# Values and denominators of the last head group moved to the head of TensorE's iteration, and the keys' lower halves made and written earlier

## The reference

```
xn  = layernorm(x)
q, k, v = relu(xn), relu(ctx), relu(ctx)            # 16 heads of 32 features
o   = softmax(q @ k.T / sqrt(32)) @ v
x   = x + tanh(g_xattn) * relu(o @ ffn_w.T + ffn_b)
xn  = layernorm(x);  xp = xn shifted by one token
r   = sigmoid((mu_r*xn + (1-mu_r)*xp) @ W_r)
k_  = relu((mu_k*xn + (1-mu_k)*xp) @ W_k) ** 2
out = x + tanh(g_ffn) * r * (k_ @ W_v)
```

## Time and profile before

| what | value |
|---|---|
| median of 3 runs | 2935.4 us (2933.75 to 2940.07) |
| the profiled execution, its time | 2935.97 us |
| its span | 2934.1 us |
| PE busy | 2833.1 us (97%) |
| PE weight loads busy | 2183.8 us (74%) |
| DVE busy | 2349.9 us (80%) |
| ACT busy | 1568.1 us (53%) |
| POOL busy | 1044.8 us (36%) |
| mean DMA rate | 139 GB/s |

### The profile page before, as it was taken

One profiled execution on the slowest core, in us unless ns is written; L12 is line 12 of the kernel. 1 busy time (PEld: TensorE's weight loads), 2 busy tenths in 40 slices (PEclk: granted clock), 3 DMA queues, 4 the chain that ended last, 5 costly groups with the idle time before them and its releaser, 6 DMA issues. The chain is left out here.

```text
span 2934.1 us, 71298 instructions
## 1 busy us (share of the span) xinstructions
PE 2833.1 (97%) x23168; PEld 2183.8 (74%) x23168; DVE 2349.9 (80%) x4175; ACT 1568.1 (53%) x2828; POOL 1044.8 (36%) x902
## 2 busy tenths in 40 slices
PE   3899999999999999999999999999999999999998
PEld 2677777777777777777777777777777777777776
DVE  5788888888888878878878878888888888888874
ACT  4455555555555555555555555555555555555552
POOL 0233333343343333333343333333333333333333
PEclk9999999999999999999999999999999999999999
DMA  5544545535445445445445445445445455355431
GB/s 167 153 129 145 154 121 151 155 121 154 151 123 156 143 127 159 138 130 159 138 131 159 133 138 155 129 145 153 126 147 156 121 152 154 122 154 149 126 104 42
DMA packets 405258, 408.56 MB, mean 139 GB/s; under 512 B 164577, under 2 KB 329441, under 8 KB 405218
## 3 DMA queue, kind: packets, MB, share of 16 engines
q1 hardware_dynamic: 352994, 340.92, 39.7%
q10 hardware_dynamic: 52224, 67.12, 7.0%
HBM read 272.64 MB, written 134.22 MB: 139 GB/s over the span
## 5 line engine op out<-in xcount | busy, mean ns | idle before, releaser
L699 DVE TENSOR_REDUCE m_nat<-bank 128x2 fp32r<-128x512 f32 x1024 | 694.6, 684 | 142.0 <-PE bank L906 141.5
L477 ACT ACTIVATE q_st<-bank 96x512 fp32r<-96x512 f32 x512 | 303.9, 593 | 765.7 <-PE bank L875 765.7
L496 ACT ACTIVATE probs<-bank 128x512 f32<-128x512 f32 x1024 | 593.6, 590 | 195.8 <-PE bank L918 187.2
L718 DVE RECIPROCAL o_val<-bank 128x256 f32<-128x256 f32 x256 | 449.3, 1755 | 60.4 <-PE bank L944 53.2
L918 PE MATMUL bank<-q_st,k_st 97*128 97x256 f32 x2048 | 437.9, 295 | 18.3 <-DMA q_st<-m_t 18.1
L906 PE MATMUL bank<-k_st,q_st 96*128 96x256 f32 x2048 | 430.0, 292 | 6.0 <-DMA k_st<-k_dram 4.5
L918 PEld LDWEIGHTS bank<-q_st,k_st 97*128 97x128 f32 x2048 | 345.5, 190 | 84.5 <-issue 22.6
L906 PEld LDWEIGHTS bank<-k_st,q_st 96*128 96x128 f32 x2048 | 356.8, 192 | 58.1 <-issue 5.9
L364 POOL TENSOR_TENSOR o_lo<-o_mv,o_hi 128x512 fp32r<-128x512 f32 x128 | 174.0, 1360 | 583.3 <-ACT o_hi L503 583.3
L397 POOL TENSOR_TENSOR xm<-xm 128x512 f32<-128x512 f32 x128 | 137.6, 1075 | 637.0 <-ACT xm L540 637.0
L708 DVE CAST m_t<-bank 4x256 fp32r<-4x256 f32 x256 | 105.1, 411 | 286.2 <-PE bank L884 286.1
(11 more groups left out here) (90 smaller groups left out, 5893.6 us busy)
## 6 DMA issues: line engine op xcount, KB each, us to landing
k_st<-k_dram SPq DMA_DIRECT2D x256, 256.0 KB, 3.6
k_raw<-ctx_t_dram SPq DMA_DIRECT2D x256, 128.0 KB, 3.1
x_ln<-x_dram SPq DMA_DIRECT2D x256, 128.0 KB
k_dram<-k_high SPq DMA_DIRECT2D x64, 512.0 KB, 3.0
k_dram<-k_raw SPq DMA_DIRECT2D x64, 512.0 KB, 4.5
k_st<-k_dram SPq DMA_DIRECT2D x256, 128.0 KB, 3.5
o_dram<-o_val SPq DMA_DIRECT2D x256, 128.0 KB, 1.7
o_mv<-o_dram SPq DMA_DIRECT2D x512, 64.0 KB, 2.0
```

Of the source, the lines that this page charges most:

```text
L477: nc.scalar.activation(q_st[0:QK, c, :, P * u:P * u + P], tp_bank[0:QK, :].rearrange("p (g t) -> p g t", g=GR), ACT.Copy).then_inc(q_stack ...
L496: nc.scalar.activation(probs[:, n // GR % 2, n % GR, :, :].rearrange("p v t -> p (v t)"), st_bank[n % 2][:, :], ACT.Exp, scale=SCALE).then ...
L699: nc.vector.tensor_reduce(m_nat[:, c % 2, :, n % GR:n % GR + 1], s_bank[n % 2][:, :].rearrange("p (u y) -> p u y", u=NU), AX_X, ALU.max, n ...
L718: nc.vector.reciprocal(o_val[:, :], pv_bank[:, T:2 * T]).then_inc(rden_ready, 1)
```

## The change

On TensorE, `values(i - 1, 3)` and `denominators(i - 1, 3)` move from around `turn(1)` into the iteration's first step, on both sides of `scores(i, 7)`. On DVE, `norm_o(i - 1, 3)` and `copy_m(i, 1)` change places, and `k_low(i + 2)` moves from the end of the iteration to the step behind `copy_m(i + 1, 0)`. On SP, `write_k(i + 2)` moves ahead of `read_o(i, 0)` and `write_o(i, 2)`. Nothing is added or removed.

```diff
@@ SP
                 move_m(i + 1, 0)
                 load_w(i)
+                write_k(i + 2, par)
                 read_o(i, 0)
                 write_o(i, 2)
-                write_k(i + 2, par)
@@ DVE
                 head_max(i, 7)
                 finish(i - 3, 1, 1 - par)
+                norm_o(i - 1, 3)
                 copy_m(i, 1)
-                norm_o(i - 1, 3)
                 mix_r(i - 2)
@@ DVE
                 head_max(i + 1, 3)
                 copy_m(i + 1, 0)
+                k_low(i + 2)
 
                 head_max(i + 1, 4)
                 stats_1(i + 2)
@@ DVE
                 head_max(i + 1, 6)
-                k_low(i + 2)
@@ TensorE
                 dense(0, 0)
+                values(i - 1, 3)
                 scores(i, 7)
+                denominators(i - 1, 3)
                 dense(0, 1)
 
                 shifted_scores(i, 1)
-                values(i - 1, 3)
                 turn(1)
-                denominators(i - 1, 3)
                 dense(0, 2)
```

## The result

The changed kernel takes 3004.97 us (median; 3003.48 to 3005.99, four runs), and the kernel before 2934.57 us beside it. The ratio is 1.0236 with a 95% interval of 1.0218 to 1.0254: 70 us slower, where 64 were forecast against the time before (3000.0 less 2936.0). The profiled execution's span is 3001.6 us instead of 2934.1.

A forecast was written before the change was run, and what follows sets the result against it. PE, busy 97% of the span, was taken to bound the kernel. 2936.0 + 112.9 (two waits) - 45.3 (`o_low`) - 4.4 (start) - 0.7 (end) + 1.5 (iteration 1) = 3000.0 us; range 2982 to 3018, 8 in 10 2965 to 3020.

The forecast's parts named there:

- First wait: PE's values would wait for DVE's `norm_o(i - 1, 2)`, delayed by the early `k_low`: 0.8 us an iteration.
- Second wait: PE's `turn(2)` would wait for DVE's `copy_m(i, 1)`, now queued behind `norm_o(i - 1, 3)`: 0.9 us an iteration.
- Borders: On PE, `scores(i, 7)` standing alone between two float32 pieces would cost 0.15 us an iteration.
- The wait that goes: PE's recurring wait for `o_low` ahead of `dense(3, 0)` would go: a gain of 45.3 us.
- SP's order: `read_o(i, 0)` behind `write_k` would cost nothing; without cover, `turn(1)` would wait for `q_st`, 1 us each making 61 us.
- Start and end: First scores at 24.1, gaining 4.4 us; last wait shrinking by 0.7; iteration 1 paying 1.5.
- The stated bounds: Range of 2982 to 3018 us, with both waits at their bounds and the start's gain open.
- Only one wait: Rival: unseen DVE slack removes one of the two PE waits, giving 2945 us; chance 0.07.
- Neither: Rival: neither PE wait on DVE shows and the kernel is faster, 2895 us; chance 0.05.
- `o_low` stays: Rival: PE's wait for `o_low` remains, so 45 us don't come back, 3045 us; chance 0.04.
- The clock falls: Rival: PE's recurring waits lower its granted clock and slow matmuls, 3150 us or more; chance 0.04.

The follow-up runs named there:

- e2: The changed kernel with `k_low` and `write_k` put back in their old places; 2953.56 us.
- e11: The changed kernel with `k_low` in two halves, one early and one in the old place, and `write_k` in its old place; 2970.00 us.
- e1: The changed kernel with `copy_m(i, 1)` put back ahead of `norm_o(i - 1, 3)` on DVE; 2990.26 us.
- e9: The changed kernel with `k_low` ahead of `copy_m(i + 1, 0)`, in DVE's idle time, and `read_o(i, 0)` ahead of `write_k` on SP; 2948.66 us.
- e5: The changed kernel with `k_low` ahead of `copy_m(i + 1, 0)`, in DVE's idle 2.06 us; 2978.61 us.
- e10: e9 with `copy_m(i, 1)` back ahead of `norm_o(i - 1, 3)` and `mix_r` moved behind `head_max(i, 8)`; 2906.97 us.
- e6: The kernel before with `k_low` and `write_k` early, but `read_o(i, 0)` ahead of `write_k` on SP; 2884.60 us.
- e3: The kernel before with only TensorE's order changed, DVE and SP as before; 2953.16 us.
- e4: The kernel before with only `k_low` and `write_k` moved as in the change, TensorE untouched; 2948.13 us.
- e8: e3 with `mix_r(i - 2)` moved behind `head_max(i, 8)` on DVE; 2945.81 us.

## Why the prediction was right

**First wait.** Right in place, count and size: 1.01 from start to start less the unwaited 0.21 is 0.80, forecast 0.8 (0.97 or 1.06 in one iteration, as the release takes 0.05 or 0.15). The edit back (e2) takes it away, half of the edit (e11) leaves 0.27.

**Second wait.** 1.035 less 0.12 is 0.915, forecast 0.9. e1 removes it. The mechanism is the forecast one, but that the size came out is in part luck: two errors of 0.1 cancel. The release was taken at 0.15 and takes 0.06; against that, L772 takes 0.84 instead of 0.75 beside POOL's late `o_low` (L364 runs from 1084.37 to 1085.66), which the sum did not have (its 0.02 for weights loaded late shows in no run by itself). Without that (e2, and e9 with the read first) the wait is 0.93 less 0.12 = 0.81. The sentence "This wait doesn't hang on the first" was too strong. With `k_low` in the idle time (e5), and so without the first wait, it is 1.25, since DVE's `finish` then falls further into POOL's `o_low`. The second wait stands without the first, but its size hangs on when POOL works.

**Borders.** 0.16 measured (e10 against e6), 0.15 forecast. The sum of the three is 0.80 + 0.915 + 0.16 = 1.875 in an iteration, forecast 1.85.

**The wait that goes.** It went, and its worth is the difference of periods between before and e6: 44.363 less 43.653 = 0.71, forecast 0.74. Both reasons that the prediction gave hold by themselves: in e2 and e3 PE's lateness hides it, in e6 the keys' earlier transfer removes it.

Closing the account: 1.875 less 0.71 is 1.165, and the period grew by 45.556 less 44.363 = 1.193, so 0.03 is not placed. The forecast was 1.11, and 61 times the 0.08 above it are 5 us, about what the time lies above the forecast.

**SP's order.** Costed at nothing as a wait of `turn(1)`, and there was none; e4 shows that it is worth 53 us as soon as `turn(1)` comes directly behind values. As a cost through POOL it was missed: some 0.1 us in an iteration, 6 us, which the shorter release hides in the sum.

**Start and end.** The first scores at 24.5 (forecast 24.1). At the first layer-norm transpose (L893) the kernel after is at 107.26 and before at 109.74, so start and first waits together gain 2.5, forecast 4.4 less 1.5 = 2.9. The end, behind the last such transpose, is 1.0 shorter (35.7 us instead of 36.7), forecast 0.7.

**The stated bounds.** "2982 to 3018" doesn't follow from the bounds named with it: 61 x 0.2 to each side for each of two waits is 24 us, so 2976 to 3024, and 3028 with the start's gain open. The 3005 measured lies in either.

**The rivals.** Only one wait: no, both are there 62 and 63 times. Neither: no. `o_low` stays: no. The clock falls: no, it is 0.997 in the mean and at 9 tenths or more in every slice, and two waits of 0.75 us in 45.6 us left it alone here. The prediction took the rule of the Trainium skill ("TensorE: Matmul & The Clock Gate", section "HAM oscillation — how this bites in real kernels") wider than it is: the loop that the section describes waits for DMA in every round for longer than it computes, which this one doesn't.

## What to carry to other kernels

Price a move on an in-order queue by the slack of what stands behind it, not by the engine's idle share: DVE was idle for a fifth of the time, but its idle time lay ahead of the moved instruction, and what was put ahead of `norm_o` or the copy reached PE in its full length less the slack there: of the 1.17 us of `k_low`, 0.80. Moving a large transfer has two sides: the small ones behind its old place gain, those behind its new place lose; here the one line order `read_o`, `write_k`, `write_o` decides between 2948 and 2885 us. And when a wait is taken away, look for the next one behind it before counting the gain: e1, e3, e4 and e8 each uncovered another.

## What the runs showed of the hardware

- **DVE beside POOL.** Means over 200 to 2800 us, first the kernel before, then e3, by line, form, count, busy time, mean ns:

```profile
L761 DVE SCALAR_TENSOR_TENSOR xd<-xd,mu_sb,xt 128x256 f32<-128x256 f32 x236 | 98.1, 477 | 0.0
L674 DVE SCALAR_TENSOR_TENSOR q_nat<-x_ln,q_nat 128x512 fp32r<-128x512 f32 x117 | 78.7, 673 | 0.0
```

```profile
L674 DVE SCALAR_TENSOR_TENSOR q_nat<-x_ln,q_nat 128x512 fp32r<-128x512 f32 x116 | 154.4, 1331 | 0.0
L761 DVE SCALAR_TENSOR_TENSOR xd<-xd,mu_sb,xt 128x256 f32<-128x256 f32 x232 | 142.0, 673 | 0.0
```

DVE's own code is the same in both. The means are 1.4 and 2 times as long, but they hide what happens: most of these instructions keep their time, and the others are held until POOL is done. Of the 232 of L761 in e3, 174 take 0.5 us and 58 take 1.3; each of the 58 began behind POOL's square (L397) and ended 0.3 behind its end. One of L674 in e3 with POOL's instruction beside it, and one in the kernel before, where DVE came first:

```profile
1039.88 2.41 DVE L674 SCALAR_TENSOR_TENSOR q_nat<-x_ln,q_nat 128x512 fp32r<-128x512 f32 x1
1039.36 2.38 POOL L390 TENSOR_TENSOR xr_lo<-xd,xr_hi 128x1024 fp32r<-128x1024 f32 x1 [0.20 <-issue]
```

```profile
1073.40 0.67 DVE L674 SCALAR_TENSOR_TENSOR q_nat<-x_ln,q_nat 128x512 fp32r<-128x512 f32 x1
1073.46 1.75 POOL L364 TENSOR_TENSOR o_lo<-o_mv,o_hi 128x512 fp32r<-128x512 f32 x1 [2.78 <-ACT o_hi L503]
```

In the second pair DVE keeps 0.67, and POOL's L364 takes 1.75 instead of the 1.29 that it has in e3. L682 takes 2.04 instead of 1.22 in e10. All these DVE instructions read two tensors of SBUF; L769, which reads one of its two from PSUM, keeps 0.68 at 1032.17 in e5 though POOL's L364 runs beside it. The Trainium skill ("GPSIMD Engine Reference", section "1. Specifications") says that GpSimd shares its SBUF interfaces with VectorE and contends with instructions that have two SBUF inputs. The rows agree, and add the size: what these instructions lose is no fixed factor, but about what is left of the other engine's instruction.
- **A small transfer behind a large one.** 128 KB written 4.55 us behind 1 MB of the same queue took 3.15 us until it could be read, and 1.73 us when 9.6 us lay between (medians over 59 iterations of the kernel before and of e6; the same reads and the same store of 512 KB are issued between the two in both).
